# Value products of two attention heads run once per pair of token tiles instead of once per tile

## The reference, cut to what matters

```
local  = softmax(q k^T * scale) @ v                 # full attention over 1024 tokens
scores = q k^T * scale; kth = top_k(scores, 102)[-1]
sparse = softmax(where(scores >= kth, scores, -1e9)) @ v
s = concat(local, sparse, memory head, prediction head) @ warboss_w + warboss_b
g = silu(relu(xn @ w1 + b1) @ w2 + b2)              # 512 -> 2048 -> 512
out = x + s * g
```

## Time and profile before

| | |
|---|---|
| median of 3 runs | 2687.07 us (2685.83 to 2688.01) |
| the profiled execution | 2687.77 us, its span 2686.0 us |
| PE busy | 2614.9 us, 97% of the span |
| DVE busy | 2298.3 us, 86% |
| ACT, POOL busy | 1401.9 us (52%), 1173.8 us (44%) |
| mean granted clock of PE | 0.994 of full speed |

### The profile page before, as it was taken

How to read it: one execution, slowest core, us unless ns; L and a number is a source line. 1 busy time by engine, 2 the same in 40 slices (tenths; PEclk the granted TensorE clock), 3 DMA queues, 4 the chain that set the end, 5 groups by cost and what they waited for, 6 DMA issues and landing times.

```text
span 2686.0 us, 42206 instructions
## 1 busy us (share of the span) xinstructions
PE 2614.9 (97%) x13476; PEld 2206.2 (82%) x13476; DVE 2298.3 (86%) x5156; ACT 1401.9 (52%) x2439; POOL 1173.8 (44%) x1059
## 2 busy tenths in 40 slices
PE   6999999799999999999999999999999999999998
PEld 5888888678888888888888888888888888888886
DVE  6555665489999998999899989998999899999996
ACT  5777767544445454444445444544444445444443
POOL 4444444323444444444444444444444444444444
PEclk9999999899999999999999999999999999999999
DMA  6777777774555455545564556455544554455544
GB/s 203 294 304 274 293 298 299 293 280 153 192 191 220 157 188 189 220 157 189 189 224 162 194 190 224 162 186 194 215 171 176 206 207 182 172 206 203 187 159 176
DMA packets 131272, 562.63 MB, mean 209 GB/s; under 512 B 14018, under 2 KB 27522, under 8 KB 89476
## 3 DMA queue, kind: packets, MB, share of 16 engines
q1 hardware_dynamic: 131076, 560.16, 56.3%
HBM read 425.90 MB, written 134.22 MB: 209 GB/s over the span
## 4 chain that ended last, share of the span: by engine, by line
PE 78%; DMA 1%; issue 0%; POOL 0%; SPq 0%; POOLq 0%; ACT 0%
PE hid L65 9%; PE hid L67 9%; PE acc L67 9%; PE hid L66 9%; PE acc L66 9%; PE acc L65 9%; PE o L1238 6%; PE scores L1224 4%; PE scores L65 2%; PE o L67 2%; PE o L66 2%; PE o L65 2%; PE scores L66 2%; PE scores L67 2%; PE o L1241 2%; DMA ffn<-ffn_scratch 1%
## 5 line engine op out<-in xcount | busy, mean ns | idle before, releaser
L1121 DVE MAX8 top_l<-larger 128x8 f32<-128x512 f32 x832 | 573.4, 689 | 13.2
L995 POOL TENSOR_TENSOR pT_s<-pT,pT_s 128x512 fp32r<-128x512 f32 x256 | 326.8, 1298 | 484.8 <-ACT pT_s L927 484.8
L995 POOL TENSOR_TENSOR h_lo<-h,h_hi 128x512 fp32r<-128x512 f32 x256 | 333.8, 1304 | 463.8 <-ACT h_hi L916 463.6
L1136 DVE MATCH_REPLACE8 larger<-top_l,larger 128x512 f32<-128x512 f32 x768 | 519.0, 676 | 0.0
L65 PE MATMUL hid<-xnT,ffn 128*128 128x512 f32 x1024 | 411.8, 402 | 6.0 <-DMA ffn<-ffn_scratch 3.6
L67 PE MATMUL hid<-xnT,ffn 128*128 128x512 f32 x1024 | 400.7, 391 | 0.0
L66 PE MATMUL hid<-xnT,ffn 128*128 128x512 f32 x1024 | 400.2, 391 | 0.0
L67 PE MATMUL acc<-ffn,h_lo 128*128 128x512 f32 x1024 | 399.5, 390 | 0.0
L66 PE MATMUL acc<-ffn,h_hi 128*128 128x512 f32 x1024 | 399.2, 390 | 0.0
L65 PE MATMUL acc<-ffn,h_hi 128*128 128x512 f32 x1024 | 398.7, 389 | 0.0
L926 ACT ACTIVATE pT<-scores 128x512 f32<-128x512 f32 x256 | 154.3, 603 | 400.5 <-PE scores L1224 400.5
(11 more groups left out here) (178 smaller groups left out, 5575.3 us busy)
## 6 DMA issues: line engine op xcount, KB each, us to landing
ffn<-ffn_scratch SPq DMA_DIRECT2D x259, 1024.0 KB, 4.9
kv<-kv_scratch SPq DMA_DIRECT2D x34, 1024.0 KB, 8.4
xnT<-xnT_scratch SPq DMA_DIRECT2D x68, 512.0 KB, 8.2
tl<-tile_scratch SPq DMA_DIRECT2D x66, 512.0 KB, 5.6
xnT_scratch<-xnT SPq DMA_DIRECT2D x16, 2048.0 KB, 12.7
kv_scratch<-kv_out SPq DMA_DIRECT2D x32, 1024.0 KB, 5.8
tile_scratch<-tiles_out SPq DMA_DIRECT2D x16, 2048.0 KB, 7.7
xin<-in_L_attn_x SPq DMA_DIRECT2D x18, 1024.0 KB, 8.3
```

The costliest lines, as they stand in the source:

```text
L995: return nc.gpsimd.tensor_tensor(out_, value, hi_.bitcast(F32), ALU.subtract).then_inc(ready, 1)
L1121: l_step = count(nc.vector.max(top_l[:, own], larger[:, :]))
L1136: l_step = count(nc.vector.match_replace(larger[:, :], top_l[:, own], larger[:, :], LOWEST))
```

## The change

The slots are put in pairs. A head's value product runs once for both tiles of a pair, with 256 columns (128 of each tile) in three passes by `product`. The sparse head of a pair runs in the even slot behind the pair, the local head in the odd slot, so that each slot from the second on has one value product of 24 matmuls where there were two of 16. The probabilities in `pT_s` now hold [block, HI or LOW, tile of the pair, 128]. Each `mix` comes one slot later (tile m-2 in slot m). The scores of one more tile stay as probabilities (`prob` has three rows), and the transposes move.

```diff
-    W_RING, TL_RING = 4, 4
+    W1_RING, W2_RING, TL_RING = 2, 4, 4
...
-        prob = sb("prob", [P, 2, S], F32)
+        prob = sb("prob", [P, 3, S], F32)
...
-        R_GATES, R_MAX, R_INVERSE, R_MIX = 2, 4, 5, 10
+        R_GATES = 2
+        R_MAX, R_INVERSE, R_MIX = (5, 3), (6, 4), (11, 7)
...
+                def load_w1(C, c):
+                    if not known_first(C, W1_RING):
+                        wait_alone(sp, f1_done, C - W1_RING + 1, sp_passed)
...
+                def load_w2(C, c):
+                    if not known_first(C, W2_RING):
+                        wait_alone(sp, f2_done, C - W2_RING + 1, sp_passed)
...
                 def slots(b):          # ACT
...
-                            head_out(2 * m - 2, 0)
-                        if some:
-                            sparse_probabilities(m - 1)
+                            sparse_probabilities(m - 1, 1 + (T - 1) % 2)
+                            transposed(m - 1, 0)
                         if T % HTILES == 0 and some:
                             gates(h - 1)
...
                         chunk(C + 1, c + 1)
...
+                        if T % 2 == 0:
+                            if some:
+                                transposed(m - 1, 1)
+                            sparse_exponents(m, T)
+                            chunk(C + 2, c + 2)
+                            local_probabilities(m)
+                            if some:
+                                head_out(m - 1, 1)
+                        else:
+                            sparse_exponents(m, T)
+                            local_probabilities(m)
+                            chunk(C + 2, c + 2)
+                            transposed(m - 1, 1)
                         chunk(C + 3, c + 3)
+                        if T % 2 == 1:
+                            head_out(m - 1, 0)
...
                 def head_out(g, unit): # PE
...
-                        if j == TILES - 1:
-                            nc.tensor.matmul(o[:, 0:P], kv[:, u, LOW, c], pT_s[:, j, 0, :], start=False, stop=False)
-                        last = nc.tensor.matmul(o[:, 0:2 * P], kv[:, u, HI, c], pT_s[:, j, :, :], start=j == 0,
-                                                stop=j == TILES - 1)
-                        if j < TILES - 1:
-                            nc.tensor.matmul(o[:, 0:P], kv[:, u, LOW, c], pT_s[:, j, 0, :], start=False, stop=False)
+                        last = product(nc, o[:, 0:2 * P], kv[:, u, HI, c], kv[:, u, LOW, c], pT_s[:, j, HI, :, :],
+                                       pT_s[:, j, LOW, :, :], j == 0, j == TILES - 1)
...
                 def slots(b):          # PE, even slots behind f1(C + 1)
...
+                                transposes(2)
+                            f2(C, c, h)
+                            f1(C + 2, c + 2, h)
...
+                            head_scores(T % TL_RING, T_QL, U_KL, sl_done)
...
+                                head_out(g, U_VS)
+                            f2(C + 1, c + 1, h)
+                            if some:
+                                pe.wait_ge(at_l, g + 1)
+                                mix(m - 2, (T - 2) % TL_RING)
+                            f1(C + 3, c + 3, h)
```

More of the change, by code:

```diff
@@ L730, in stage2 @@
         inv = sb("inv", [P, 2], F32)
-        prob = sb("prob", [P, 2, S], F32)
+        prob = sb("prob", [P, 3, S], F32)
         pT = sb("pT", [P, 2, 512], F32)
[L733 to L738, removed]
+        pT_s = sb("pT_s", [P, TILES, 2, 2, P], F32R)
+        at = sb("at", [P, 2 * P], F32)
+        at_hi = sb("at_hi", [P, 2, 2 * P], F32R)
+        at_lo = sb("at_lo", [P, 2, 2 * P], F32R)
+        mixed = sb("mixed", [P, 2, D], F32)
         gate = sb("gate", [P, HTILES, D], F32)
@@ L832, in _ @@
                 load_kv(U_KS, 0)
-                load_ffn(0, 0)
+                load_w1(0, 0)
                 load_xn(0, 0, 0)
-                load_ffn(1, 1)
+                load_w1(1, 1)
                 load_kv(U_KL, 0)
-                load_ffn(2, 2)
+                for c in range(W2_RING - 1):
+                    load_w2(c, c)
                 load_tl(1, 1, 1)
@@ L926, in transposed, with head_out @@
                         nc.scalar.activation(pT[:, j, :], scores[:, c], ACT.Copy)
-                        nc.scalar.activation(pT_s[:, j * HTILES:(j + 1) * HTILES, 0, :],
+                        nc.scalar.activation(pT_s[:, j * HTILES:(j + 1) * HTILES, HI, t, :],
                                              scores[:, c].rearrange("p (t n) -> p t n", n=P), ACT.Copy)\
                             .then_inc(pT_h, 1)
[L931 to L935, removed]
+                def head_out(g, head):
+                    act.wait_ge(pv_done, g + 1)
+                    if not known_first(g, 1):
+                        act.wait_ge(at_l, g)
+                    nc.scalar.activation(at[:, :], o[:, 0:2 * P], ACT.Copy)
+                    nc.scalar.activation(at_hi[:, head, :], o[:, 0:2 * P], ACT.Copy).then_inc(at_h, 1)
                 def gates(h):
@@ L1004, in transposed, with head_out @@
                         half = slice(j * HTILES, (j + 1) * HTILES)
[L1005 to L1012, removed]
+                        lo(pT_s[:, half, LOW, t, :], pT[:, j, :].rearrange("p (t n) -> p t n", n=P),
+                           pT_s[:, half, HI, t, :], pT_l)
+                def head_out(g, head):
+                    pool.wait_ge(at_h, g + 1)
+                    lo(at_lo[:, head, :], at[:, :], at_hi[:, head, :], at_l)
                 def residual(m, T):
@@ L1046, in _ @@
                     slots(b)
[L1047 to L1054, removed]
+                last = B * TILES - 1
+                transposed(last, 0)
+                transposed(last, 1)
+                residual(last - 3, TILES - 4)
+                head_out(last, 1)
+                for T in range(HTILES + 1, TILES):
+                    residual((B - 1) * TILES + T, T)
             @block.vector
@@ L1125, in search @@
                             s_step = count(nc.vector.max(top_s[:, own_s], smaller[:, :]))
-                        if r == R_MIX and not known_first(m, 1):
-                            mix(m - 1, (T - 1) % HTILES)
+                        if r == r_mix and not known_first(m, 2):
+                            mix(m - 2, (T - 2) % HTILES)
                         if r == R_GATES:
@@ L1218, in head_scores, with transposes @@
                     last.then_inc(done, 1)
-                def transposes(i, head):
-                    pe.wait_ge(pr_ready, i + 1)
+                def transposes(own):
                     for j in range(TILES):
-                        last = nc.tensor.transpose(scores[:, j * P:(j + 1) * P], prob[:, head, j * P:(j + 1) * P],
+                        last = nc.tensor.transpose(scores[:, j * P:(j + 1) * P], prob[:, own, j * P:(j + 1) * P],
                                                    ident[:, :])
@@ L1253, in mix @@
                     for j in range(2):
-                        product(nc, o[:, :], at_hi[:, j, :], at_lo[:, j, :], ww_hi[:, j, :], ww_lo[:, j, :],
+                        product(nc, o[:, :], at_hi[:, j, n], at_lo[:, j, n], ww_hi[:, j, :], ww_lo[:, j, :],
                                 j == 0, False)
```

269 lines of the change are left out of this document (154 added, 115 removed).

## The result

The changed kernel takes 2711.34 us (median of 4 runs, 2708.49 to 2713.35) against 2686.83 before. The ratio is 1.0088, with a 95% interval of 1.0075 to 1.0101: slower by 24.5 us.

What follows compares the result with a forecast made beforehand. PE's list of matmuls was taken as the bound. Value products -53.9, waits of `mix` +66, clock +12, start +5 and tail +4.7 gave +34 us on 2687.1, so 2721 us, range 2698 to 2742.

Steps and rivals of the forecast that it cites:

- value products, 62 slots: PE's value products in stage 2: 3.68 us per slot becomes 2.81, a gain of 0.87, 53.9 us in all.
- waits of `mix`, even slots: PE's `mix` waits for POOL's `at_lo`: 1.2 us at T = 2 and 6, 2.1 at T = 4, 4.3 at T = 0; 66 us.
- clock: PE's matmuls fall to half clock after waits of over 2 us, 1.6 us lost each; 12 us.
- start, up to slot 2: Start of stage 2: chunk 2's first weight lands late, delaying slot 0's scores and search; 4 us, 5 with a cold start.
- tail: Behind the last slot: ACT copies both heads ahead of the gates, first residual ends at 12.5 us instead of 7.6; 4.7 us.
- eight falls: Half-clock stretches on PE expected after 6 of the 7 waits at T = 0 and 2 of the 8 at T = 4.
- link by link walk: Even slots: row maximum, DVE's inverse, ACT's scaling and copies, POOL's `at_lo`, then PE's `mix`; each link timed from the earlier trace.
- T = 0: Slots at the loop's turn: DVE's search begins at 5.0 us, `at_lo` is ready at 29.0; 4.3 us of wait in all.
- transfer term: Start of stage 2: chunk 2's first weight is the 10th MB, landing at about 560, where PE wants it at 552.
- DVE's load as the bound: Rival: DVE's waits for `sl` and ACT add to its load, every slot 33 us or more; 2725 to 2740, 5%.
- "faster" rival: Rival: the chain behind DVE's inverse hides, DVE or ACT 2 us ahead; 2683, or 2643 with T = 0 hidden too; 10%.
- 0.115 each: PE's old value products: a head's 16 matmuls take 1.84 us, 0.115 each, the 128-column ones too, so narrow ones save nothing.

Runs made afterwards that it cites:

- early copies: Against the changed kernel, in even slots ACT copies the sparse head's value product between the local exponentials and their scaling; 2652.4 us, ratio 0.987 to the kernel before.
- late mix: Against the changed kernel, PE's `mix` in even slots is put behind f1(C+3) instead of ahead of it; 2654.43 us, ratio 0.9877 to the kernel before.
- DVE work ahead of the inverse: Changed kernel plus two needless DVE row maxima (about 0.6 us each) just ahead of the inverse in even slots; 2778.08 us, ratio 1.0345 to the kernel before.
- two passes: Changed kernel with the lo*hi pass (low part of v) of the value products left out; 2718.19 us, ratio 1.0115 to the kernel before.
- two start experiments: On the early copies: batch 0's value loads put behind first weights of chunks 2 and 3, 2648.12 us; on top, slot 0's local scores first on PE, 2640.8 us.
- DVE work behind the inverse: Changed kernel plus the same two needless DVE row maxima just behind the inverse in even slots; 2708.95 us, ratio 1.0089 to the kernel before.

## Why the prediction was right, and where its terms were off

The forecast was slower, at 2721 (2698 to 2742); it is 2711.3. Point by point, on the spans:

| term | predicted | found |
|---|---|---|
| value products, 62 slots | -53.9 | -46.5 |
| waits of `mix`, even slots | +66 | +52 |
| clock | +12 | +3 |
| start, up to slot 2 | +5 | +8.8 |
| tail | +4.7 | +3.7 |
| turn of the loop | none | -1.3 |
| sum | +34 | +19.8 |

The found terms are read from the lengths of slots, first `ss` to first `ss`. The direction and the mechanism were forecast. The size came nearer than its terms deserve: the gain was put 7 us too high and the waits and the clock together 23 too high, which partly cancel; the total is 14 too high. Two small slips are in the working as well: the tail's 12.5 less 7.6 is 4.9, not 4.7, and eight falls of 1.6 are 12.8, not 12.

**Value products.** In the rows above a head takes 1831.47 - 1828.58 = 2.89 us, not 2.81: the passes are up to 0.12 apart. That is a gain of 0.79. Slots without a wait are 32.07 long where they were 32.82 (31.96 was predicted), so 0.75 of it arrives: 62 x 0.75 = 46.5.

**The chain.** The link by link walk was right. `mix` starts 1835.36 - 1810.44 = 24.92 us into slot T = 6, against 24.9 predicted; at T = 4, whose first `ss` is at 1743.32, it is 26.68 against 26.7. The early copies, the late mix and the DVE work ahead of the inverse show the chain from three sides, not just its presence in the trace.

**T = 0 was mis-sized.** Its `mix` starts at 1104.14 - 1076.84 = 27.3, not 29.0, and f2(C) doesn't wait for the gates. DVE's search begins 3.35 us into the slot instead of 5.0:

```profile
1078.43 1.28 DVE L1107 SCALAR_TENSOR_TENSOR prob<-sc,kth,prob 128x1024 f32<-128x1024 f32 x1 [3.15 <-issue]
...
1080.19 0.69 DVE L1160 TENSOR_TENSOR larger<-sc 128x512 f32<-128x512 f32 x1 [0.23 <-DVE top_s L1210]
```

I carried the 4.13 us of the loop's turn over from the earlier trace rows; here it took 3.15, and DVE came to it earlier. The seven waits are 1.8 to 3.0 us, 15 in all where I had 30. The waits at all T, 45.0 us of idle without the tail's, are delays of 52 by the slots' lengths (19 at T = 2 and 6, where 19 were predicted, 16 at T = 4 for 17, and 17 at T = 0 for 30): after a wait the next start follows 0.34 us on and not 0.23, and the idle is counted only from the modelled end of the last matmul. A slot T = 2 is 33.29 long with its wait of 0.97, and 32.07 with the early copies.

**The clock was mis-sized.** I expected eight falls. In the change two even slots show one. After the T = 4 wait of 1.78 us at 703.33 matmuls are 0.43 apart, and the granted clock from 704.7 to 707.7 is 0.50:

```profile
704.77 0.63 PE L67 MATMUL o<-ww_hi,at_lo 128*128 128x512 f32 x1
705.19 0.63 PE L65 MATMUL o<-ww_hi,tl 128*128 128x512 f32 x1
```

The next `mix` comes at 770.22, 66.9 us on, where the same distance elsewhere is 1568.46 - 1503.10 = 65.36: 1.5 us lost per fall. Of the 16 waits of 0.97 us none was followed by such a stretch, of the 11 of 1.8 to 1.9 one, of the 4 of 2.2 to 3.0 one. With the DVE work ahead it was 13 of 16 behind waits of 2.15 us, but only 9 of 15 behind those of 2.9 to 4.2, so the length of the wait alone doesn't tell; what else does is open. The page "TensorE: Matmul & The Clock Gate" of the Trainium skill (section "HAM oscillation — how this bites in real kernels") tells of a kernel whose bursts of matmuls, between transfer waits of about 3 to 5 us, each start cold. The prediction quoted it without the length of those waits. The change, with some 60 us of work between its waits, doesn't show it (2 of 31); the kernels with the DVE work ahead (22 of 31) and with two passes (18 of 31) come much nearer, with waits of 2 to 4 us.

**The start was mis-sized.** The transfer term was right (the weight landed at 558.6, predicted 560). The wait of slot 1 behind it was larger than I had worked out, and the clock too: in slots 0 and 1, 26 matmuls are 0.43 apart where 11 were, 3 us of the 8.8. The two start experiments begin slot 2 6.4 us and 5.2 us sooner, which is all of it and 2.7 us more.

**Open.** Why a slot is 0.75 us shorter when its value product is 0.79 shorter wasn't looked into. What puts DVE's turn of the loop at 3.15 or 4.13 us wasn't tried either.

The rivals: DVE's load as the bound is out by the DVE work behind the inverse, which cost nothing. The "faster" rival named the right condition (the chain 2 us shorter); the early copies fulfil it and land at 2652, with the start and tail losses still in.

## What to carry to other kernels

When a change saves work on the engine that is the bound, look at the first thing that engine will wait for once it gets there sooner, and follow it back through the in-order lists of the other engines: here a finished result lay behind an unrelated instruction on ACT that waited for a third engine, and moving two copies ahead of it turned +24.5 us into -35. A wait can be taken away at either end, by making the producer earlier or by putting other work of the waiting engine over it. Where a slot ends in a wait that recurs, shortening the work ahead of the wait buys nothing in that slot, and a longer wait can cost the clock on top.

## What the runs showed of the hardware

- Matmuls of 256 columns in three passes follow each other every 0.117 to 0.12 us, twice as often as 512-column ones (0.23), and a 256- and 128-column pair before took 0.23 as well, as long as two 256-column ones. The prediction's "0.115 each" is the mean of such a pair.
- In the change, with waits of 0.97 to 3.0 us, PE's clock fell behind 2 of 31; with about 1.2 us more on each (83.1 us in 32 waits) behind 22 of 31. It was low for some 79 us more, and the kernel lost 67 us where the waits alone were 36.5. With two passes instead of three (18 of 31) less work made the kernel slower.
- The turn of the loop held DVE for 2.9 to 3.3 us in the changed kernel and 3.5 to 4.2 in the one before (6 turns each), PE for 0.3 to 1.4 and 0.8 to 1.6.
